# A DLRM tower on one core: the tenth step of every chunk (step 9) computed from a rounded and a residual product, its residual made by GpSimd

## The reference

```python
def _L0_rec_ref(inputs, w0, w1, w2, b0, b1, b2):
    x0 = inputs                       # [2048, 39, 16]
    xk = inputs
    for idx, (W, b) in enumerate(params):
        z = jnp.einsum('bhd,bkd,hks->bsd', x0, xk, W) + b[None, :, None]
        z = jax.nn.relu(z)
        if idx != n_layers - 1:
            half = z.shape[1] // 2
            xk = z[:, :half, :]
            direct.append(z[:, half:, :])
        else:
            direct.append(z)
    return jnp.sum(jnp.concatenate(direct, axis=1), axis=-1)
...
e = jnp.stack([tbl_0[ids[:, 0]], ..., tbl_38[ids[:, 38]]], axis=1)
h = jnp.concatenate([z, dense_ctx], axis=1)
h = jnp.maximum(h @ W_top1 + b_top1, 0.0)
h = jnp.maximum(h @ W_top2 + b_top2, 0.0)
y = h @ W_top3
```

## Time and profile before

| | us |
|---|---|
| median of 3 runs | 2478.97 (2478.65 to 2479.06) |
| the profiled execution | 2477.58, span 2475.8 |
| TensorE busy | 2422.1 (98%) |
| VectorE busy | 2211.2 (89%) |
| GpSimd busy | 1948.6 (79%) |
| ScalarE busy | 1724.4 (70%) |

### The profile page before, as it was taken

One profiled execution on the slowest core, in us unless ns is written; L12 is line 12 of the kernel. 1 busy time (PEld: TensorE's weight loads), 2 busy tenths in 40 slices (PEclk: granted clock), 3 DMA queues, 4 the chain that ended last, 5 costly groups with the idle time before them and its releaser, 6 DMA issues.

```text
span 2475.8 us, 33269 instructions
## 1 busy us (share of the span) xinstructions
PE 2422.1 (98%) x8854; PEld 1640.9 (66%) x8854; DVE 2211.2 (89%) x1876; ACT 1724.4 (70%) x2185; POOL 1948.6 (79%) x1331
## 2 busy tenths in 40 slices
PE   5999999999999999999999999999999999999989
PEld 2566666666666666666666666666666666666655
DVE  1599999999989999999999999899999999999990
ACT  1677777777767777767777776676777777677663
POOL 6688888888878888888888888788888888865550
PEclk9899999999999999999999999999999999999999
DMA  3778667766856766776686677577668667766830
GB/s 74 157 145 175 141 138 160 158 137 141 175 124 139 174 134 140 163 157 137 144 172 138 139 161 160 121 157 160 137 139 174 145 139 154 164 136 134 171 84 0
DMA packets 214716, 352.60 MB, mean 142 GB/s; under 512 B 34382, under 2 KB 47566, under 8 KB 214588
## 3 DMA queue, kind: packets, MB, share of 16 engines
q1 hardware_dynamic: 194717, 347.07, 65.4%
q0 software_dynamic: 19968, 5.15, 2.1%
HBM read 346.97 MB, written 5.12 MB: 142 GB/s over the span
## 4 chain that ended last, share of the span: by engine, by line
PE 54%; POOL 26%; issue 14%; DVE 4%; ACT 1%; POOLq 0%; DMA 0%; ACTq 0%; DVEq 0%
PE ps L858 20%; POOL Pl L397 11%; POOL emb L391 11%; PE ps L868 11%; PE ps L848 10%; PE ps L836 8%; PE ps L831 2%; POOL dir L426 2%; DVE P L731 1%; DVE ps L731 1%; DVE Pl L736 1%; PE ps L983 1%; POOL sqx L403 1%; PE ps L975 1%; PE ps L824 1%
## 5 line engine op out<-in xcount | busy, mean ns | idle before, releaser
L397 POOL TENSOR_TENSOR Pl<-P,Ph 128x1024 fp32r<-128x1024 f32 x448 | 1074.8, 2399 | 285.3 <-ACT Ph L541 261.5
L858 PE MATMUL ps<-Ph,wh 128*128 128x512 f32 x2048 | 965.2, 471 | 9.9 <-ACT Ph L541 9.9
L541 ACT ACTIVATE Ph<-ps 128x1024 fp32r<-128x1024 f32 x576 | 590.3, 1025 | 406.7 <-DVE ps L731 393.0
L731 DVE TENSOR_TENSOR P<-xb,ps 128x1024 f32<-128x1024 f32 x704 | 853.2, 1212 | 2.8 <-DMA xb<-x_dram 2.8
L736 DVE TENSOR_TENSOR Pl<-ps,Ph 128x1024 fp32r<-128x1024 f32 x576 | 705.1, 1224 | 116.1 <-ACT Ph L541 97.4
L858 PE MATMUL ps<-Ph,wl 128*128 128x512 f32 x1920 | 755.5, 393 | 0.0
L868 PE MATMUL ps<-Pl,wh 128*128 128x512 f32 x2048 | 742.2, 443 | 7.4 <-POOL Pl L397 7.4
L391 POOL DMA_INDIRECT emb<-tbl_in,idx x624 | 600.6, 962 | 170.5 <-issue 145.0
L731 DVE TENSOR_TENSOR ps<-xb,ps 128x1024 f32<-128x1024 f32 x576 | 707.1, 1228 | 28.5 <-issue 9.4
L541 ACT ACTIVATE Ph<-P 128x1024 fp32r<-128x1024 f32 x448 | 473.9, 1058 | 186.1 <-DVE P L731 129.8
L868 PEld LDWEIGHTS ps<-Pl,wh 128*128 128x128 f32 x2048 | 384.3, 188 | 200.0 <-issue 118.2
(11 more groups left out here) (68 smaller groups left out, 857.2 us busy)
## 6 DMA issues: line engine op xcount, KB each, us to landing
xb<-x_dram SPq DMA_DIRECT2D x1280, 256.0 KB
emb<-tbl_in,idx POOLq DMA_INDIRECT x624
x_dram<-rows SPq DMA_DIRECT2D x64, 78.0 KB
xb<-w_in SPq DMA_DIRECT2D x16, 128.0 KB
xb<-wt_in SPq DMA_DIRECT2D x2, 512.0 KB, 4.4
xb<-dense_in SPq DMA_DIRECT2D x1, 768.0 KB, 5.3
wp<-w_in SPq DMA_DIRECT2D x4, 128.0 KB
xb<-w0a_in SPq DMA_DIRECT2D x1, 448.0 KB
```

The costliest lines, as they stand in the source:

```text
L397: pool.tensor_tensor(Pl[:, h_slot(ref, c, k)], P[:, p_slot(ref, c, k)], Ph[:, h_slot(ref, c, k)], ALU.subtract).then_inc(low_pool, 1)
L541: act.activation(Ph[:, h_slot(ref, c, k)], p, ACT.Copy).then_inc(rounded, 1)
L731: dve.tensor_tensor(p, xb[:, x], xk.unsqueeze(1).broadcast_to([128, 2, N]), ALU.mult)\
L858: pe.matmul(z_of(c, k), w[:, q, j, :], Ph[:, h_slot(ref, c, k), j, :], start=k in (L1B, L2) and i + j == 0, stop=False)
```

## The change

Step 9's letter goes from P to G. One plain step less, one split step more in every chunk: 3 plain and 17 split steps. The weights of that step move from the plain store `wp` to the split stores `wh` and `wl`; lists and ring positions that are derived from `KIND` follow. Since step 9 is the last step that runs ahead of the first chunk and is now split, its residual is still outstanding when the first tile begins; `late` is handed over to it.

```diff
-KIND = "GVPVGPVGVPVGVGVGVGVP"
+KIND = "GVPVGPVGVGVGVGVGVGVP"
...
-            assert not late
-
-            def tile(T, ref, first=False, last=False):
-                late = None
+
+            def tile(T, ref, late=None, last=False):
...
-            tile(0, 0, first=True)
+            tile(0, 0, late)
             with pe.Fori(1, TILES - 1) as T:
                 tile(T, 1)
             tile(TILES - 1, TILES - 1, last=True)
```

## The result

The changed kernel takes 2544.12 us (median of 4 runs, 2541.22 to 2548.32); the kernel before, run beside it, 2478.81 (2476.69 to 2479.06). The ratio is 1.0265, 95% interval [1.0253, 1.0278]: 65 us more, where I had said 2.6. All but some 10 us of that come from a place of which the prediction does not speak: the code of ScalarE's tile loop.

A forecast was written before the change was run, and what follows sets the result against it. TensorE, busy 98%, was taken to bound the kernel, with GpSimd's arrears taking its gain: 14 intervals +4.3, six splits outside -1.7, sum +2.6 on the profiled 2477.58, 2480.2; the median's 1.39 more gives 2481.6, forecast 2481.5, range 2472 to 2490.

The forecast's parts named there:

- The step that failed: ScalarE, step 9 of each chunk: one added rounding of about 1 us finds time there and costs nothing.
- TensorE's 3.86 us for steps 9 and 10: TensorE, each chunk: steps 9 and 10 take 3.86 us instead of 4.21, 0.35 us less.
- The walk along GpSimd: GpSimd from second chunk's step 17: added residuals cost 2.34 and 2.27 us; TensorE 0.64, then 0.53 us late at step 0.
- L403 (here L404) now holds TensorE's L838 (L841): Sign in the new profile: L403 appears as releaser of L838 in the second and third chunk.
- The size of an interval: From one tile's second chunk to the next tile's: +0.31 us, 14 times, +4.3 us.
- the make-up of the loop: Loop of VectorE and ScalarE: L553, waiting for nothing new, starts 0.05 us after the activation before, making up 0.22 us a chunk.
- The edges: Six added splits outside the 14 intervals, at the start and the end: each pays 0.22 to 0.35 us, together -1.7.
- The third: Rival, slower: later roundings make GpSimd wait again at the fourth chunk's step 17, up to 8.4 us more, 2489.9; chance 0.28.
- The second: Rival, the gain stays: GpSimd free by each chunk's step 0, VectorE's loop decides, 13.6 us less, 2465.3; chance 0.12.
- The rule weighed: GpSimd's residual: 2250 ns by the skill's figure instead of the row's 2399, giving 2477.4 in all; the row was taken.

The follow-up runs named there:

- e8: Changed kernel, ScalarE's loop moved 90 places, GpSimd's step 9 residual cut to 8 of each 512 columns in tiles 1 to 13: 2473.44 us, ratio 0.9978.
- e1: Kernel before, ScalarE's tile loop moved by 20 places with idle semaphore increments ahead of it: 2528.96 us, ratio 1.0206.
- e2: Changed kernel, ScalarE's tile loop moved by 90 places with idle semaphore increments ahead of it: 2489.51 us, ratio 1.0048.
- e10: Changed kernel, ScalarE's loop moved 90 places, one gather per tile moved from the third chunk's step 12 to the first chunk's step 8: 2472.38 us, ratio 0.9980.
- e4: Changed kernel, ScalarE's tile loop moved by 40 places with idle semaphore increments ahead of it: 2533.77 us, ratio 1.0222.
- e3: Kernel before, ScalarE's tile loop moved by 90 places with idle semaphore increments ahead of it: 2478.50 us, ratio 0.9997.
- e5: Kernel before, ScalarE's tile loop moved by 170 places with idle semaphore increments ahead of it: 2534.11 us, a single run.
- e9: Kernel before, ScalarE's tile loop moved by 250 places with idle semaphore increments ahead of it: 2484.15 us, a single run.
- e11: Kernel before, ScalarE's loop moved 90 places, one gather per tile moved from the third chunk's step 12 to the first chunk's step 8: 2476.55 us, ratio 0.9992.

## Why the prediction was wrong

**The step that failed** is this: "ScalarE gets one rounding of about 1 us per chunk; at step 9 it now has time, ... I cost it at nothing." For the rounding's microsecond the evidence agrees: where GpSimd's work is taken out, the kernel is faster than before (e8). But the step costed what ScalarE executes and not the code that it executes it from. Twelve instructions more in the loop and ten ahead of it moved the loop across one block end more, and each of 13 returns costs 4.2 us on the average, 54.6 in all. Nothing in the prediction bounded that, nor was any rival of this kind; the view to look at, queue 14 of the page, would have shown 16 blocks and no reload, and e1 shows that the kernel before stood within 20 places of the same fault.

The other steps are judged on e2, where the reload is gone. Its 2489.51 is 8.0 above the 2481.5 that I forecast, and lies in my range by 0.5 us.

**TensorE's 3.86 us for steps 9 and 10: right.** In the changed kernel:

```profile
1309.10 0.40 PE L831 MATMUL ps<-x,sel 78*128 78x512 f32 x1
...
1312.97 0.39 PE L831 MATMUL ps<-x,sel 78*128 78x512 f32 x1
...
1316.83 0.39 PE L831 MATMUL ps<-x,sel 78*128 78x512 f32 x1
```

1312.97 to 1316.83 is 3.86, where the earlier trace rows had 4.21.

**The walk along GpSimd: right.** GpSimd's rows of e2, second chunk's step 17, then steps 11 and 17 of the third chunk, steps 0, 11 and 17 of the fourth, step 0 of the next first one; and TensorE's low pair of step 0 in the three chunks:

```profile
1328.34 2.40 POOL L398 TENSOR_TENSOR Pl<-P,Ph 128x1024 fp32r<-128x1024 f32 x1 [1.84 <-ACT Ph L544]
...
1354.34 2.41 POOL L398 TENSOR_TENSOR Pl<-P,Ph 128x1024 fp32r<-128x1024 f32 x1
...
1365.00 2.43 POOL L398 TENSOR_TENSOR Pl<-P,Ph 128x1024 fp32r<-128x1024 f32 x1
...
1371.02 2.42 POOL L398 TENSOR_TENSOR Pl<-P,Ph 128x1024 fp32r<-128x1024 f32 x1
...
1390.28 2.41 POOL L398 TENSOR_TENSOR Pl<-P,Ph 128x1024 fp32r<-128x1024 f32 x1
...
1400.57 2.38 POOL L398 TENSOR_TENSOR Pl<-P,Ph 128x1024 fp32r<-128x1024 f32 x1
...
1406.96 2.41 POOL L398 TENSOR_TENSOR Pl<-P,Ph 128x1024 fp32r<-128x1024 f32 x1
```

```profile
1336.75 0.74 PE L871 MATMUL ps<-Pl,wh 128*128 128x512 f32 x2
...
1373.49 0.73 PE L871 MATMUL ps<-Pl,wh 128*128 128x512 f32 x2
...
1409.43 0.73 PE L871 MATMUL ps<-Pl,wh 128*128 128x512 f32 x2
```

Each row less 1328.34, and the row less 1324.73, gives the lateness: third chunk step 11: 26.00 - 24.32 = 1.68 (I said 1.72), step 17: 36.66 - 35.22 = 1.44 (1.43). Fourth chunk, TensorE: 45.15 - 44.53 = 0.62 (0.64); GpSimd's step 11: 1.63 (1.58), step 17: 1.03 (0.98). Next first chunk, TensorE: 81.09 - 80.52 = 0.57 (0.53). None of these residuals but the first waits for its rounding, and a pair that starts in the record of TensorE right at its residual's end stands in all three chunks. L403 (here L404) now holds TensorE's L838 (L841), as said; in the kernel before it did so for 0.2 us in all:

```profile
PEld ps L841 <- POOL sqx L404: 21.6, 29, 0.9
```

**The size of an interval: too small.** I said +0.31 us a tile, e2 has 144.8 against 144.2, +0.58. TensorE is 0.57 late in the next first chunk, L553 (here L556) 0.67 there, 0.48 in the second chunk, and step 17 behind it 0.53. I had assumed that L553 is late by what TensorE is, and that the loop of VectorE and ScalarE makes up 0.22 in a chunk. ScalarE's rows of e2, L556 in the fourth chunk and in the next first one, show what holds:

```profile
1381.38 0.68 ACT L556 ACTIVATE dir<-ps,bias 64x512 f32<-64x512 f32 x1 [0.65 <-PE ps L871]
...
1416.13 1.06 ACT L544 ACTIVATE Ph<-P 128x1024 fp32r<-128x1024 f32 x1
1417.32 0.68 ACT L556 ACTIVATE dir<-ps,bias 64x512 f32<-64x512 f32 x1
```

In the fourth chunk L553 waits for TensorE and comes 0.73 late. In the next first chunk it waits for nothing: the loop itself is still late, and has made up 0.06, with L556 starting 0.13 us after the rounding ahead of it and not 0.05. In the second chunk it makes up 0.19. With GpSimd out of the way (e8) the tile gained 144.2 - 143.8 = 0.4, 0.1 a chunk. So the make-up of the loop, resting on the 0.05 us estimated for an activation that waits for nothing new, is the term that was mis-sized: 0.22 a chunk by my sum, 0.06, 0.19 and 0.1 as measured. Times 14 the 0.27 by which the interval is too small are 3.8 us of the 7.9 by which +10.5 exceeds +2.6.

**The edges: not seen.** In e2's second tile ScalarE waits 3.18 us for gathered rows, which it did not do before, the tile being 147.4 us and not 144.8:

```profile
303.84 0.73 ACT L517 ACTIVATE emb_h<-emb 128x624 fp32r<-128x624 f32 x1 [3.18 <-DMA emb<-tbl_in,idx]
```

The residuals at the start, which I counted as paying, delay the gathers that follow them: e8, whose residuals of step 9 are short from tile 1 on, has no such wait, the changed kernel (2.97) and e10 (3.31) have it. And GpSimd stands for 5.13 us ahead of a gather in the 13th tile, which takes 149.7 us:

```profile
1978.26 0.94 POOL L392 DMA_INDIRECT emb<-tbl_in,idx  x1 [5.13 <-issue]
```

Every trace has pauses of this kind ahead of a gather, three or four over 3 us; the kernel before has 3.23, 6.41, 4.47 and 3.12, of which the last does not lengthen its tile (144.2). The last pause goes with the change: it is 5.13 to 5.41 in the three traces that have all the residuals and the old places of the gathers (e2, e4, the changed kernel), 3.12 to 3.21 in before, e1, e3, e5, e8 and e9, and absent in e10 and e11. So some 5 us of e2's excess, and of what moving the gather won, are this pause. These are one trace each, and what GpSimd does in such a pause no row shows.

**The rivals.** The third, slower with 2489.9, comes within 0.4 us of e2, but not by its mechanism: GpSimd does not wait at the fourth chunk's step 17 (1400.57 above). The second, that the gain stays, holds only once GpSimd's arrears are removed (e8, e10), and then gives some 5 us, not 13.6, because VectorE's loop gives 0.1 a chunk. **The rule weighed** against GpSimd's row, 2250 ns estimated from the Trainium skill's figure (GPSIMD Engine Reference, section 3.1), is borne out no better after: the group of the changed kernel says 2405.

```profile
L397 POOL TENSOR_TENSOR Pl<-P,Ph 128x1024 fp32r<-128x1024 f32 x512 | 1231.5, 2405 | 201.4 <-ACT Ph L541 190.9 <-issue 4.7
```

## What to carry to other kernels

When a change lengthens or moves the body of a hardware loop, look at the queue that loads instructions and at "issue" waits at the loop's edge, and if they grow, shift the loop by idle instructions where the engine waits anyway before judging the change itself: here that separated 54.6 us of code loading from 10.5 us of the change. And before giving an engine that is "79% busy" more work, walk its queue with the slack at each wait: the walk was right to 0.05 us, and it also says which item to move (one gather, worth 17 us here, some 5 of them a pause that the walk did not have), provided that what is moved keeps its own deadline.

## What the runs showed of the hardware that I had not expected

- A jump back in ScalarE's program takes 0.24 us, or 6 to 8 us (4.8 and 4.9 in two cases), with a body of 318 or 330 instructions, depending on where it stands; a miss loads some five blocks of 8 KB in each pass ((82 - 17) / 13).
- Of the five engines only ScalarE's jumps back were slow here; TensorE's body, some 1250 to 1290 records long, returned in at most 0.23 us in every run.
- After 2.76 us without work TensorE ran at a granted clock of 0.52 for some 3 us, that is at 1.2 GHz, and its matmuls followed each other at 0.43 us and not 0.23; behind six of the thirteen returns the clock did not fall.
